# Running the down projection of a sweep before the next sweep's normalization in an eight-core FFN kernel

## The reference

```python
def fp4_quant_dequant(x):            # blocks of 16 along the last dim
    scale = jnp.maximum(jnp.max(jnp.abs(xb), axis=-1, keepdims=True) / 6.0, 1e-12)
    idx = jnp.searchsorted(_MID, jnp.abs(xb / scale))
    q = _GRID[idx] * jnp.sign(xn) * scale
def _L0_ffn_ref(x, w_gate, w_up, w_down):       # 1024 -> 2816 -> 1024
    h = jax.nn.silu(fp4_linear(x, w_gate)) * fp4_linear(x, w_up)
    return fp4_linear(h, w_down)
x = x + 0.5 * _L0_ffn_ref(_layernorm(x), w_gate, w_up, w_down)
x = x + _L0_attn_ref(_layernorm(x), ...)
x = x + 0.5 * _L0_ffn_ref(_layernorm(x), w_gate, w_up, w_down)
```

## Time and profile before

| what | us |
|---|---|
| three executions | 11758.16, 11801.05, 11941.37 |
| their median | 11801.05 |
| the profiled execution | 11758.16 |
| its span on core 7, the slowest core | 11755.7 |
| its spans on the other cores | 11471.8 to 11754.8 |

### The profile page before, as it was taken

How to read it: one execution, slowest core, us unless ns; L and a number is a source line. 1 busy time by engine, 2 the same in 40 slices (tenths; PEclk the granted TensorE clock), 3 DMA queues, 4 the chain that set the end, 5 groups by cost and what they waited for, 6 DMA issues and landing times.

```text
span 11755.7 us, 109490 instructions; the slowest of 8 cores (11471.8 to 11755.7 us)
## 1 busy us (share of the span) xinstructions
PE 6257.0 (53%) x39392; PEld 4461.7 (38%) x39392; DVE 4207.3 (36%) x5019; ACT 1840.4 (16%) x4812; POOL 2053.5 (17%) x1030
## 2 busy tenths in 40 slices
PE   0221222756747475774748654455555456647477
PEld 0121212443626254362535533333333343526254
DVE  6667664141323314132241312222232341323322
ACT  1111112021111112011120111111101120211111
POOL 2233322121212112021221200000000121212121
PEclk6555555877778676776767775555555678878788
DMA  1221221423223131321314220000000223223143
GB/s 48 59 63 46 52 49 30 93 46 80 54 65 65 36 83 39 80 54 46 76 29 91 43 58 8 11 13 15 22 18 18 52 46 80 54 69 64 46 83 70
DMA packets 1855411, 604.17 MB, mean 51 GB/s; under 512 B 1800353, under 2 KB 1803938, under 8 KB 1853858
## 3 DMA queue, kind: packets, MB, share of 16 engines
q1 hardware_dynamic: 1699106, 529.01, 20.3%
q10 hardware_dynamic: 155776, 68.17, 2.0%
HBM read 528.85 MB, written 68.16 MB: 51 GB/s over the span
## 4 chain that ended last, share of the span: by engine, by line
PE 41%; DVE 23%; DVEq 10%; issue 8%; ACT 7%; POOL 5%; DMA 3%; POOLq 2%; SPq 1%; ACTq 1%
PE ps L560 19%; PE ps L640 12%; PE ps L719 6%; DVE scr L258 5%; DVEq L239 3%; DVE scr L250 3%; DVE scr L284 2%; DVE sm_m L236 2%; DVEq L267 2%; POOLq L300 2%; POOL sp_l L302 2%; ACT scr L292 2%; POOL sp_h L301 1%; DVE scr L280 1%; DVE scr L268 1%
## 5 line engine op out<-in xcount | busy, mean ns | idle before, releaser
L560 PE MATMUL ps<-wcol,xqT 128*128 128x256 bf16 x25344 | 3211.1, 297 | 1200.1 <-ACT xres L576 1011.1
L560 PEld LDWEIGHTS ps<-wcol,xqT 128*128 128x128 bf16 x25344 | 2678.1, 106 | 1722.8 <-issue 1225.7
L236 DVE TENSOR_REDUCE sm_m<-hb_all 128x128 f32<-128x2048 f32 x96 | 206.7, 2153 | 4683.8 <-POOL hb_all L582 4681.4
L298 POOL TENSOR_TENSOR sp_l<-scr,sp_h 128x2048 bf16<-128x2048 f32 (+1 forms) x134 | 502.5, 3750 | 6236.4 <-ACT scr L292 6236.4
L640 PE MATMUL ps<-wdn,hqT 128*128 128x512 bf16 x6336 | 1515.7, 407 | 123.0 <-DMA wdn<-stash_d 102.6
L354 PE MATMUL ps<-c_idb_s,sp_h 128*128 128x128 bf16 x912 | 110.6, 307 | 2604.5 <-POOL sp_l L302 2595.5
L354 PEld LDWEIGHTS ps<-c_idb_s,sp_h 128*128 128x128 bf16 x912 | 90.6, 140 | 2624.0 <-issue 2624.0
L258 DVE TENSOR_SCALAR scr<-scr 128x2048 bf16<-128x2048 f32 (+2 forms) x938 | 1023.0, 1139 | 42.0 <-issue 2.9
L640 PEld LDWEIGHTS ps<-wdn,hqT 128*128 128x128 bf16 x6336 | 651.8, 103 | 983.3 <-issue 521.0
L719 PE MATMUL ps<-hqT 128*128 128x128 f32 x1536 | 511.9, 467 | 388.9 <-DVE hqT L722 154.4
L582 POOL TENSOR_TENSOR hb_all<-hsilu,xres 128x256 f32<-128x256 f32 x528 | 390.4, 745 | 1777.4 <-ACT xres L576 1777.4
(11 more groups left out here) (114 smaller groups left out, 5042.0 us busy)
## 6 DMA issues: line engine op xcount, KB each, us to landing
wcol<-stash_g SPq DMA_DIRECT2D x528, 256.0 KB, 4.7
wcol<-stash_u SPq DMA_DIRECT2D x528, 256.0 KB, 5.1
wdn<-stash_d SPq DMA_DIRECT2D x1056, 128.0 KB, 2.4
xin<-xall SPq DMA_DIRECT2D x32, 512.0 KB, 4.7
xres<-xall SPq DMA_DIRECT2D x64, 256.0 KB, 3.5
xin<-wg SPq DMA_DIRECT2D x22, 512.0 KB, 4.2
xin<-wu SPq DMA_DIRECT2D x22, 512.0 KB, 3.8
stash_g<-stg ACTq DMA_DIRECT2D x44, 256.0 KB, 2.6
```

The costliest lines, as they stand in the source:

```text
L236: V.tensor_reduce(out=mb[:, :nb], in_=v3, axis=AX.X, op=AL.max, apply_absolute_value=True)
L298: G.tensor_tensor(out=sp_l[:, :F], in0=t2[:, :F], in1=sp_h[:, :F], op=AL.subtract)
L560: mm = T.matmul(reg, xqT[si][xh_][:, dc, :], wb[wh_][:, mi2, dc, :], start=(k == 0), stop=(k == np_ * DCH - 1))
```

## The change

In `emit_ffn`, the call of `emit_down` for the current sweep is moved ahead of the call of `emit_pre` for the next one. Each engine's stream changes accordingly: in those of SP, ACT, GpSimd, DVE and TensorE alike, what `emit_down` emits now stands before what `emit_pre` emits.

```diff
                     emit_gateup(stiles, side if sw == 0 else None)
+                    emit_down(stiles)
                     if sw + 1 < nsw:
                         emit_pre(tiles[(sw + 1) * SWEEP:(sw + 2) * SWEEP])
-                    emit_down(stiles)
                 wait_all_stores(SY)
```

## The result

| | kernel before | changed kernel |
|---|---|---|
| median of 14 executions each, us | 11,805.6 | 11,726.1 |
| lowest and highest | 11,638 to 12,021 | 11,434 to 11,884 |
| profiled execution, span of the slowest core | 11,755.7 | 11,622.1 |
| ratio of the compared executions | | 0.9644, 95% interval 0.9561 to 0.9728 |

The account below looks back on a forecast made before the run. No engine was taken to bound the whole; core 7 set the time. Each boundary would fall from 163.55 to 155.5 us, 8.05 less, times ten 80: 11,721 us on the median, range 11,570 to 11,860.

Parts of the forecast that it names:

- the wcol waits: Gate/up's ten waits for wcol behind down, 18.75 us each; forecast to disappear with wcol loaded under pre.
- the xin path: From down's last matmul to pre's first Square: xin issue, landing and DVE work, forecast to end last, at +10.6 us.
- part 6: The clock at each boundary: two slow starts before, two after; counted as nothing, with 2.6 us to either side.
- How the numbers follow: Closing step with the chances: forecast 0.62, faster 0.12, same 0.85, slower 0.03; 2% taken as 236 us.
- same: The outcome that the whole kernel's time changes by less than 2%, 236 us; chance 0.85.
- B: Rival: denser matmuls spread the throttle to more sweeps; three more give 11,889 us, six more 12,057; chance 0.08.
- C: Rival: the slower die's throttle falls away, 274 + 80 us lower, 11,447 us on the median; chance 0.11.
- a sign: Sign that the forecast is wrong: a die's median moves by over 100 us at another granted clock.
- Lost cover: Gate/up's wait for wcol at a boundary: without pre to cover the loads it would cost 18.75 us again.

Follow-up runs that it names:

- e5: Changed kernel with pre's first two xin loads issued ahead of down's loads; its one unthrottled die had a median of 11,405.1 us.
- e4: Changed kernel with pre split in halves emitted around down's halves and wcol loads spread between wdn loads; median 10,630.3 us.
- e8: The changed kernel a third time, in alternation with the kernel before; medians 11,581.5 us changed and 11,682.3 us before.
- e3: Changed kernel with the wcol loads held until pre's last copy to xqT is done; ratio to the kernel before 1.0128.
- denser kernels: Changed kernel with pre split under down's halves, median 10,630.3 us; and that kernel with the second half's first wdn loads issued earlier, 10,438.8 us.
- e2: Kernel before, its order kept, with the next sweep's first two wcol loads issued ahead of down's loads; median 11,454.1 us, ratio 0.9814.

## Why the prediction was right, and where it failed

**The mechanism held.** Down starts 30.4 us after gate/up (forecast 30.1); the wcol waits vanished; the Square starts at +11.0 (10.6); from there to gate/up it is 115.0 (114.8); DVE does nothing in down; wcol is issued at +18. That ACT's evictions keep pre's first Square from starting under down, with SP's place for xin adding 2 us, is shown by e5 (floor at +9.0, with DVE idle for 149 us behind ACT) and e4 (1,118 us when the order lets them overlap).

**The sum was 14 us too large: 80 forecast, 65.6 measured on unthrottled dies.** The means over all boundaries, from the first and last matmul of each part on core 1 before and core 5 after:

| term, us | before | after | times | effect |
|---|---|---|---|---|
| gate/up to down | 144.8 | 30.45 | 10 | |
| down to gate/up | 18.6 | 125.9 | 10 | with the row above -71 |
| first half of down | 58.5 | 59.8 | 12 | +15 |
| second half of down | 59.4 | 59.7 | 12 | +3 |
| gate/up after the first sweep | 360.3 | 359.4 | 11 | -10 |

The first two rows give 7.1 per boundary where I had 8.05: 0.4 from the gap of 30.4, 0.5 from the xin path. The third is part 6, "I count nothing", and here misled me: it showed a start of down at 0.50 behind the pause of 145 us, and I took it for all of them. On core 1 down's first half started at full clock in four of the ten boundaries (57.1 to 57.4 us); over cores 0 to 3 it was 22 of 40, while in the changed kernel, after 30 us of pause, none did on any unthrottled core. Gate/up got a part of it back: it starts at full clock in 7 of 40 cases on cores 4 to 7, before in none. In both cases the full starts came where pre's transposes stood right ahead; but they stood ahead of the slow starts as well, so what decides isn't shown. Both effects lie inside the 2.6 us either way. The four add up to 63 us.

**The step that failed is the last one, the chances.** Under "How the numbers follow" I took 2% for about what a measurement of this kernel can tell, and the chance of 0.85 for "same" rests on that. I took the throttle as something that might spread (B) or fall away (C) with the change, gave C 0.11, and carried a ratio from one profiled execution to a median. But the profile already had the two levels side by side, 11,482 and 11,756 in one execution. The time of either kernel is the larger of two dies, each with an excess of 0 to some 400 us from execution to execution. So a comparison of short series can miss by more than 2% whatever the change does, and the first one did: 0.9644, where the unthrottled dies say 0.9943. 11,447 was the time I gave for C, and 11,434 and 11,442 came up, in the two executions of 14 where neither die had an excess. The forecast of C had the time and not the cause: no later series shows that the order lowered anything. The 3.6% did not return in two further series (0.9955 and 0.9935), and the shares of unthrottled dies, 41% and 39%, can't be told apart.

**The median was luck.** 11,726 lies 5 us from the forecast of 11,721, but the changed kernel's medians in three series were 11,726, 11,628 and 11,581, and those of the kernel before in four 11,806, 11,717, 11,682 and 11,632. The forecast had a sign for this among its own: a die's median that moves by over 100 us at another granted clock. Both dies did (11,482 to 11,610 and 11,751 to 11,416), and between executions of the unchanged kernel they do so too.

**Rival B and the Trainium skill's rule.** The rule cited with B (the Trainium skill, TensorE: Matmul & The Clock Gate, "Seeing it yourself": a third core with dense matmuls brings the die to 13/16 for as long as the load lasts) would have every die at that level in the dense stages of every execution, in both kernels. 72 of the 180 dies counted stayed with the unthrottled crowd; where such a die was recorded (die 0 of the kernel before, die 1 of the changed one, both of e8), its cores spent 0 to 31 us at 0.81, against 1,640 to 2,395 us on the other die of the first two. The excess of a die goes with that time: 1,640 to 1,779 us at 0.81 made a die 193 us longer than its neighbour, 2,301 to 2,395 us made it 269, both 0.11 to 0.12 us per us. The order of the parts shows no effect on it that these series could tell, so B at the price I gave it, 168 us for three more throttled sweeps, is out too.

**Lost cover.** I priced it at 18.75 us; in e3 it was 12.3 of gap. Of the 19, 3.5 were SP's delay, and the loads took 15.5 beside other traffic and 12.1 alone.

Open: what makes a die fall to the lower level in one execution and not in the next. The denser kernels had 5 of 16 and 1 of 8 dies unthrottled, fewer than 40%, but too few to say that density matters.

## What to carry to other kernels

Where one queue issues all loads in program order, a wait for data may be a matter of place: moving two calls of the load function ahead of a stage (e2, 212 us) was worth three times as much as moving the stage itself (66 us), which pays for its cover with evictions that were free. Before expecting two stages on different engines to overlap, look at each engine that both use and that works in order: its part of the later stage has to be emitted ahead of its last instruction that waits for the earlier one. Here that was ACT, and splitting the stage gave 1,118 us. And when the cores of one execution already stand at two levels, compare dies at the same level before believing a ratio of a few per cent.

## What the runs showed of the hardware

- How long a die is granted only 0.81 differs from die to die and from execution to execution of one program: 41% and 39% of dies escaped it in two kernels with the same work, and the excess of the others reached 350 and 420 us of 11,500. Where traces were kept of both kinds in one execution it was 0.11 to 0.12 us per us spent at 0.81.
- A pause costs more than its length: gate/up's first 5 us had 49 matmuls at a granted clock of 1.00 without a pause, and 25 at 0.50 (the 1.2 GHz level) behind 19 us of waiting. Over the whole of gate/up it was 1.6 us on average.
- A stage can start at the full clock behind a long, mostly idle stretch: in the kernel before, 22 of the 40 first halves on cores 0 to 3 that stood behind 145 us with only transposes on TensorE took 56.9 to 57.4 us, the other 18 took 58.7 to 59.3. The transposes ended right ahead of all 40, so they alone don't decide it.
- Eight wcol loads of 256 KB took 12.1 us when issued alone and 15.5 us when the stores and the last residual load ran beside them.
